# Projected keys, queries and values split before they are stored, and all heads of a swapped tile turned by the scratch

## What is computed

```python
def attn(q, w_qkv, w_dense):                 # 32 heads, 8 key/value heads, 128 wide
    qkv = q @ w_qkv.T
    qs, ks, vs = jnp.split(qkv, np.cumsum(SPLITS)[:-1], axis=-1)
    qh = qs.reshape(Bq, Sq, KVHEADS, G, HEAD_D)
    scores = jnp.einsum('bskgd,btkd->bkgst', qh, kh) * scale
    scores = jnp.where(causal, scores, jnp.finfo(scores.dtype).min)
    probs = jax.nn.softmax(scores, axis=-1)
    attn = jnp.einsum('bkgst,btkd->bskgd', probs, vh)
    return attn.reshape(Bq, Sq, NHEADS * HEAD_D) @ w_dense.T

x = x + _layernorm(attn(_layernorm(x), w_qkv, w_dense))
x = x + _layernorm(ffn(_layernorm(x)))       # gate, up, silu, down over 1792, block-quantised
```

## Time and profile before

| | us |
|---|---|
| median of 3 runs (lowest, highest) | 1168.42 (1166.78, 1168.89) |
| the profiled execution's own time | 1167.88 |
| its span, first to last instruction | 1166.1 |
| mean granted clock of TensorE, of full speed | 0.994 |

### The profile page before, as it was taken

The page is one execution under the profiler, slowest core; times in us unless marked ns, Lnnn a source line. Parts: engine busy times, 40 slices in busy tenths (PEclk is TensorE's granted clock), DMA queues, the critical chain, the costliest instruction groups (busy, mean ns, idle before and its releaser), DMA issues.

```text
span 1166.1 us, 17549 instructions
## 1 busy us (share of the span) xinstructions
PE 1136.8 (97%) x5618; PEld 953.9 (82%) x5618; DVE 838.6 (72%) x1935; ACT 602.5 (52%) x1300; POOL 750.5 (64%) x829
## 2 busy tenths in 40 slices
PE   8999999999999999999999999999999899999996
PEld 7878888878887888888888888887887688888884
DVE  5545455457888798888888988887667955665568
ACT  6532324236766667767767677665678521111111
POOL 7844456435764865856848659566775676677636
PEclk9999999999999999999999999999999999999998
DMA  6443555325466576485584765865120011110101
GB/s 219 136 154 148 189 205 189 153 93 193 133 205 204 161 233 193 138 275 167 179 255 147 220 196 157 267 180 182 50 73 1 1 55 55 55 42 12 54 0 72
DMA packets 122097, 164.43 MB, mean 141 GB/s; under 512 B 10400, under 2 KB 95904, under 8 KB 118688
## 3 DMA queue, kind: packets, MB, share of 16 engines
q1 hardware_dynamic: 122016, 163.44, 43.3%
HBM read 98.78 MB, written 64.62 MB: 140 GB/s over the span
## 4 chain that ended last, share of the span: by engine, by line
PE 90%; DVE 5%; ACT 2%; DMA 1%; issue 1%; POOL 0%; DVEq 0%; ACTq 0%; POOLq 0%; SPq 0%
PE psS L1404 27%; PE psOY L1531 17%; PE psOY L1404 15%; PE psOY L1546 14%; PE psT L1404 11%; PE psT L1509 5%; PE psS L1567 1%; DVE pT_lo L1098 1%; DVE y L1242 1%; DVE oT_lo L1098 1%; ACT oT_hi L1068 0%; PE psS L1410 0%; ACT pT_hi L941 0%; DVE square L1182 0%; DVE amax L1227 0%
## 5 line engine op out<-in xcount | busy, mean ns | idle before, releaser
L697 POOL TENSOR_SCALAR probs_long<-probs_long,rsum 128x896 f32<-128x896 f32 (+9 forms) x124 | 128.0, 1033 | 82.4 <-DVE rsum L1169 81.4
L951 ACT ACTIVATE probs_long<-probs_long,negmax 128x896 f32<-128x896 f32 (+9 forms) x124 | 121.2, 978 | 51.6 <-DVE negmax L1163 51.2
L697 POOL TENSOR_SCALAR probs_short<-probs_short,rsum 128x416 f32<-128x416 f32 (+15 forms) x128 | 80.6, 637 | 104.0 <-DVE rsum L1169 101.9
L1404 PE MATMUL psS<-kT_hi,qT_hi 128*128 128x256 f32 (+8 forms) x384 | 136.2, 355 | 2.9 <-DVE negmax L1163 2.9
L1404 PE MATMUL psS<-kT_hi,qT_lo 128*128 128x256 f32 (+8 forms) x384 | 128.5, 335 | 0.0
L1404 PE MATMUL psS<-kT_lo,qT_hi 128*128 128x256 f32 (+8 forms) x384 | 128.5, 335 | 0.0
L1546 PE MATMUL psOY<-wd_hi,oT_hi 128*128 128x512 f32 x256 | 107.2, 419 | 3.5 <-DVE oT_lo L1098 2.7
L638 POOL TENSOR_TENSOR qT_lo<-q_raw,qT_hi 128x512 fp32r<-128x512 f32 x64 | 86.4, 1350 | 22.5 <-ACT qT_hi L935 22.5
L1546 PE MATMUL psOY<-wd_hi,oT_lo 128*128 128x512 f32 x256 | 100.8, 394 | 0.0
L1546 PE MATMUL psOY<-wd_lo,oT_hi 128*128 128x512 f32 x256 | 100.6, 393 | 0.0
L1531 PE MATMUL psOY<-pT_hi,v_hi 128*128 128x512 f32 x222 | 91.6, 413 | 1.8 <-DVE pT_lo L1098 1.8
(11 more groups left out here) (185 smaller groups left out, 3301.5 us busy)
## 6 DMA issues: line engine op xcount, KB each, us to landing
q_raw<-q_scr SPq DMA_DIRECT2D x64, 256.0 KB, 3.6
p_scr<-probs_long SPq DMA_DIRECT2D x24, 512.0 KB, 3.3
probs_long<-p_scr SPq DMA_DIRECT2D x96, 128.0 KB, 3.6
raw<-in_w_qk SPq DMA_DIRECT2D x10, 1024.0 KB, 5.7
p_scr<-probs_long SPq DMA_DIRECT2D x21, 448.0 KB, 3.0
probs_long<-p_scr SPq DMA_DIRECT2D x84, 112.0 KB, 3.3
q_scr<-cB SPq DMA_DIRECT2D x16, 512.0 KB, 2.6
q_scr<-cA SPq DMA_DIRECT2D x16, 512.0 KB, 2.6
```

The source lines that it names most:

```text
L697: nc.gpsimd.tensor_scalar(row, row, rsum[:, column(t, h)], 1.0, ALU.mult, ALU.mult).then_inc(p_ready, 1)
L951: nc.scalar.activation(row, row, ACT.Exp, bias=negmax[:, column(t, h)], scale=-1.0, accum_out=lsum[:, column(t, h)]).then_inc(e_done, 1)
L1404: last = nc.tensor.matmul(dst, a, b, start=(start and k == 0), stop=(stop and k == len(terms) - 1), skip_group_check=resumed)
```

## The change

1. *Split at the source.* In the projection ACT writes the high part of every piece (`hi_of_c`), and DVE (`lo_of_c11`, `lo_of_sums`) or POOL (`lo_of_c12`) the low part, into tiles `made`; values likewise (`take_values`, `lo_of_values`). All scratch arrays hold two float32-sized parts, so stores and loads of keys, queries and values move twice the bytes. PE's P1 of the next quad waits for `c11_done`, and each product for the factor it uses alone.
2. *No restoring.* RKV and RQ are gone on ACT and POOL. Loads go straight into `kT`, `v` and `qT`, and PE waits for the DMAs. A tile's queries are four DMAs in pieces of 64 columns instead of one in pieces of 128. Since `qT` has three buffers, a load waits for the last scores of tile t - 3.
3. *A quad of queries* now holds two heads of one group with the two halves' columns alternating in blocks of 32.
4. *All four heads* of every swapped tile are exchanged (87 heads become 108), and POOL makes the low parts of two of them.
5. All four tables of moves are new.

The diff, cut to its core:

```diff
-    SWAPS = {4: (3, 2, 1), 5: (3, 2, 1), 6: (3, 2, 1), 7: (3, 2, 1, 0)}
-    POOL_LOW = {4: (), 5: (), 6: (), 7: (3,)}
+    SWAPS = {4: (3, 2, 1, 0), 5: (3, 2, 1, 0), 6: (3, 2, 1, 0), 7: (3, 2, 1, 0)}
+    POOL_LOW = {4: (3, 2), 5: (3, 2), 6: (3, 2), 7: (3, 2)}
...
-    PE_MOVES = {("P",): 0.6, ("P", 0, 0, 0): -15.9, ("P", 0, 0, 1): -11.4, ("P", 0, 0, 2): -12.6, ("P", 0, 0, 3): -4.4,
+    PE_MOVES = {("P", 0, 0, 0): -10.4, ("P", 0, 0, 1): -9.8, ("P", 0, 0, 2): -8.6, ("P", 0, 0, 3): -9.3, ("PV", 0, 0): 3.5,
...
             def load_q(t):
-                g, i = t // NT, TILES[t]
-                sp.dma_start(q_raw[t % 2][:].rearrange("p (b q) -> p b q", b=HG),
-                             q_scr[g * HG:(g + 1) * HG, :, i * P:(i + 1) * P].transpose([1, 0, 2])).then_inc(q_in[t % 2], 16)
+                (g, i), per = (t // NT, TILES[t]), HG * P // 2
+                half, cols = i // TPB, slice(i % TPB * per, (i % TPB + 1) * per)
+                for part in range(2):
+                    tile = qT[t % 3][part][:].bitcast(F32).rearrange("p (u h c) -> p u h c", u=HG, h=2)
+                    for pair in range(2):
+                        sp.dma_start(tile[:, :, pair, :], q_scr[g, pair, part, half, :, cols].rearrange(
+                            "p (u c) -> p u c", u=HG)).then_inc(q_in[t % 3], 16)
...
-                sp.wait_ge(q_lo, t - 1)
+                sp.wait_ge(s_full, LAST_SCORE[t - 3] + 1)
                 load_q(t)
                 if n == 4 and g + 1 < G:
                     if g >= 1:
                         sp.wait_ge(o_full, g * NT)
-                    load_kv(g + 1)
+                    load_keys(g + 1)
+                    load_group_values(g + 1)
...
-            def restore_q(t):
-                pool.wait_ge(q_hi, t + 1)
-                hi, lo = (from_units(u) for u in qT[t % 3])
-                low(lo, by_head(q_raw[t % 2]), hi).then_inc(q_lo, 1)
+            def lo_of_c12(q):
+                pool.wait_ge(c_hi, 4 * q + 4)
+                low(made_piece(q, 1, 1, 0), in_spans(c12[:]), made_piece(q, 0, 1, 0)).then_inc(c12_done, 1)
...
+            def hi_of_sums(q):
+                for k, (half, x, source) in enumerate(((1, 1, c22), (0, 1, c21), (1, 0, c12))):
+                    act.wait_ge(w_done, 5 * q + 3 + k)
+                    if k == 0 and q >= 2:
+                        act.wait_ge(made_out[q % 2][1], 32 * (q // 2))
+                    hi_of_c(q, half, x, source[:])
...
                 nc.vector.tensor_tensor(u3[:], quad_bank[2], u2[:], ALU.add).then_inc(w_done, 1)
+                lo_of_c11(q)
...
-                        pe.wait_ge(a_done, 2 * q)
+                        pe.wait_ge(c11_done, q)
...
-                    pe.wait_ge(q_lo, t + 1)
+                    pe.wait_ge(q_in[t % 3], 64 * (t // 3 + 1))
```

More of the change, by code:

```diff
@@ L453, in x_rows, with made_tile, made_piece, in_spans @@
             return t[:, first:first + KT, i % TPB * P:(i % TPB + 1) * P]
-        def restored(e, piece):
-            if piece < 2:
-                return [t[:, piece * BANK:(piece + 1) * BANK] for t in kT[e]]
-            return [t[:, (piece - 2) * TPB:(piece - 1) * TPB, :] for t in v[e]]
+        def made_tile(q, part, half):
+            return last_made[part, half] if q == QUADS - 1 and (part, half) in last_made else made[q % 2][part][half]
+        def made_piece(q, part, half, x):
+            tile = made_tile(q, part, half)
+            if q < KEY_QUADS:
+                return tile[:, x * BANK:(x + 1) * BANK].rearrange("p (n q) -> p n q", q=SPAN)
+            return tile[:].rearrange("p (n x q) -> p n x q", x=2, q=SPAN)[:, :, x, :]
+        def in_spans(tile):
+            return tile.rearrange("p (n q) -> p n q", q=SPAN)
         def from_units(tile):
@@ L585, in _ @@
                     load_dense(0)
-            sp.wait_ge(outA, 16 * QUADS)
-            sp.wait_ge(outB, 16 * QUADS)
-            for t in range(2, T):
+            for e in range(2):
+                for half in range(2):
+                    sp.wait_ge(made_out[e][half], 32 * (QUADS // 2))
+            for t in range(3, T):
                 g, n = divmod(t, NT)
@@ L823, in _ @@
                     weight_blocks(n)
-                for piece in FIRST_KV.get(q, ()):
-                    restore_kv(0, piece)
-                if q in FIRST_Q:
-                    restore_q(FIRST_Q[q])
+                if q >= 1:
+                    lo_of_c12(q - 1)
                 if q >= QUADS - 4 + 1 and q < QUADS - 1:
@@ L836, in _ @@
                 norm_head(0, h)
+            lo_of_c12(QUADS - 1)
             pool.wait_ge(p_full, 7 * QUADS)
```

264 lines of the change are left out of this document (147 added, 117 removed), and 99 rows, old and new, of tables (ACT_MOVES, DVE_MOVES, PE_MOVES, POOL_MOVES).

## The result

The changed kernel takes **1212.76 us** (1210.26 to 1215.96 in 4 runs) against 1167.60 us for the kernel before (1166.63 to 1168.89 in 4 runs): ratio 1.0388, 95% interval 1.0359 to 1.0416. It is slower by 3.9%. The forecast was 1160.0 with a range of 1149 to 1188.

A forecast was written before the change was run, and what follows sets the result against it. The prediction took TensorE (busy 97% of the span) as the bound, with DMA the resource to watch. Its terms, -13.8 + 2.1 - 1.2 - 2 + 7 = -7.9 us, took 1167.9 to 1160.0 us, range 1149 to 1188.

The forecast's parts named there:

- Transposes and scores: TensorE in the attention: 126 transposes removed, 13.8 us off; scores of those heads in two halves, 2.1 us on.
- The helpers: DVE, POOL and ACT in the attention: their moved work stays covered by PE and gets looser, 0 us.
- The projection: Projection stage: added splits on DVE, ACT and POOL and doubled scratch writes (DMA share 0.76) fit, 0 us.
- The first copy: Projection: the first product copy no longer waits for stored values, taking 1.2 us off PE.
- The stall at 371 us: Attention: one 2.3 us PE wait and its slow clock may go in the new order; 2 us off, between 0 and 4.0.
- DMA in the attention: Attention transfers: exchanges, keys, values and 256-byte query packets raise the 16 engines' time from 335 to 482 us.
- share 0.92, which fits, barely: Attention: 482 us of transfers in a stretch of 526 us, taken to fit on the DMA engines.
- It fits too: SP's queue: 143 us of added issues against 245 us in which SP waited for heads from GpSimd.
- New waits: Attention: the exchange behind each load of keys and values comes late, 1 us in each of seven groups, 7 us on.
- SP waiting some 100 us for POOL: Sign in the new profile: SP's queue still waits some 100 us for POOL if the forecast holds.
- rival A: Attention: exchange late in every group, 4 us each plus slow clock, 40 us instead of 7; 1193 us, chance 0.18.
- B: Rival: 256-byte query packets cost 30 ns each, attention transfers 581 us at share near 1; 1210 to 1254 us, chance 0.07.

## Why the prediction was wrong

- *Transposes and scores, -11.7 us.* Right where it can be seen alone: 9.5 us of time, 12.9 of PE's busy time. How it divides stays open: the transposes' group fell by 20.6 us (38.7 to 18.1), more than the 13.8 forecast, but the groups overlap, since a matmul is shown longer than its distance to the next (0.37 for 0.21 us in the earlier trace rows), and they do not add up to the 12.9.
- *The helpers, 0.* In the attention their own work stayed covered: without the low loads PE waits 1.1 us for maximum and queries. But DVE got heavier than forecast: by the terms its busy time should rise by 21 us in all (-32 in the attention, 20 x 2.1 and 16 x 0.68 before it), and it rose by 43.1 (838.6 to 881.7).
- *The projection, 0.* It cost 3.2 us: PE was busy 136.81 of 140 us where it had no gap, and it waited 3.1 us for `c`. The share came out at 0.78 for the forecast 0.76. With three heads and no low loads, what is left of the change costs 4.9 us.
- *The first copy, -1.2 us.* The wait is gone, as forecast.
- *The stall at 371 us, -2.* Six longer ones stand where it stood. In the version without low loads it is gone: granted clock 1.00 in all of 262 to 850 us.
- *DMA in the attention.* The amount was right. The forecast added 147 us of the 16 engines' time in the attention (335 to 482) and 20 x 2.8 + 15 = 71 in the projection, 218 in all; the queue's time rose from 505 to 744, by 239. So was the packet price, 17 ns taken and 18.6 measured. **The step that failed is the sentence behind it, "share 0.92, which fits, barely", and its partner for SP's queue, "It fits too".** Both compare a sum of work with a length of time. But an exchange is a chain of two transfers, with a wait for the landing in between, and the scores wait for its end. What is under way when it starts is added to it. With all four heads exchanged, SP's waits for transfers away came to 51.5 us without the low loads and to 112.8 with them, and DVE's waits for rows coming back to 4.1 and 64.3. The mean share (0.73 and 0.84) does not show it: around the group loads it is 1.04 for 15 us, and the forecast had seen the same saturation in the earlier trace rows.
- *New waits, +7 us.* The mechanism was named at its place and sized too small: 1 us in each of seven groups, where one wait of 1.4 and six of 2.6 to 3.7 us stood (the six are 19.2 us), and the forecast counted no clock for them, which cost some 10 us more than before. What no term held is the rest: some 17 us of waits for maximum and queries, most of them far from a group load, with only query loads in front. The query loads, 1 MB for each pair of tiles, were costed as filling of the queue and not as delay of the exchange behind them, and leaving out their low parts alone gives back 38.9 us.
- *What would show it.* Of the signs, "SP waiting some 100 us for POOL" failed (15.1 us), and so did PE's busy time; "long waits there, or a granted clock under 1" is what came, the sign of rival A.
- *The rivals.* A was right in kind. Its 40 us for the late exchanges with their clock was even above the 19.2 us of the six stalls and the 12 us that the clock cost (half of 23.9), and its 1193 us is short by the waits at query loads, the projection and what has no row. B is excluded: the share stayed at 0.84, and 131072 packets of 256 bytes averaged 18.6 ns in the trace (those of 512 bytes 28.2 ns), far from B's 30 ns. That its range (1210 to 1254) holds the measured time is chance.

The account of the 45.8 us between the two spans: 30.6 more for the maximum, 4.0 for queries, 3 to 5 for the projection and the rest of the split, 2.0 for `oT_lo`, and (23.9 - 3.4) / 2 = 10 for the lower clock between 262 and 850 us, less 9.5 to 12.9 for the heads. (23.9 and 3.4 us are the times at the lower clock in this stretch, after and before.) That is 37 to 42; some 4 to 9 us have no row of their own. They lie in PE's busy time, which is 19.0 us above that of the version without low loads (1146.1 to 1127.1), 10 to 12 of them by the clock. Why the rest came is open.

No version here with the whole computation in it is faster than the kernel before. The one at 0.9963 leaves the low parts out.

## What to carry to other kernels

When a change adds transfers, don't ask whether the sum of transfer time fits under the span; ask which transfer an engine waits for, what stands in front of it when it starts, and add that to its chain. Two edits that each look right can spoil one another through such a chain: here the fourth exchange was worth 9.5 us with room on the DMA engines and cost 16.7 us without. And a long queue wait for work (245 us for GpSimd) is slack only at the places where it stands, not a budget for additions elsewhere.

## What the runs showed of the hardware

- Small packets: 256 bytes 18.6 ns each, 512 bytes 28.2 ns (means over all packets of these sizes in the changed kernel's trace; the 512-byte ones are stores there, and the 512-byte query loads of the kernel before, in its attention, took 28.5 ns). Per byte the small ones cost a third more, and replacing them by 1024-byte ones gave 14.4 us, their shorter issues included. The Trainium skill (DMA: Bandwidth & Descriptors, Specifications) has a read-modify-write below 512 bytes; a packet here got cheaper, not dearer, so no such step shows.
- An issue of query loads from SP took about 0.5 us for 512 packets (two 1.06 us). Two of 1024 packets took 1.06 us too, but four of them in a row 3.66. Behind a group's loads two issues took up to 5.87 us, and up to 8.07 us where the group's 3 MB had been issued from ScalarE's queue.
- Stalls of PE of 2.6 to 3.7 us were followed by a granted clock of 0.50 (1.2 GHz) for 3.4 or 6.8 us in five of six cases. In the version without low loads, whose waits in the attention are 1.4 us at most, it stayed at 1.00.
